# First stage of a four-layer network: five items of the side work move up one step, the sums and taps are dealt out anew

## The reference

```python
u        = layernorm(x_proj)                 # over channels, per token
x_in, z  = split(u @ in_w + in_b)            # 128 and 128 channels
xc       = silu(conv1d_3(x_in))              # three taps along the tokens
dt, B, C = split(xc @ xproj_w)               # 4, 16 and 16 numbers per token
dt       = softplus(dt @ dt_w + dt_b)        # 128 channels
h[n]     = exp(dt * A[n]) * h[n] + (dt * xc) * B[n]     # n = 0..15, a scan over tokens
y        = sum_n C[n] * h[n] + D * xc
out      = (y * silu(z)) @ out_w             # then the 3x3 convolution's half is added, ReLU, residual
```

## Time and profile before

| what | value |
|---|---|
| median of 3 runs | 6879.02 us (6876.97 to 6880.95) |
| span of the profiled execution | 7648.3 us, 89071 instructions |
| own time of the profiled execution | not recorded apart from its span |
| first stage in it, first to last gated product | 141.0 to 2121.3 us |
| busy over the span | TensorE 75%, VectorE 72%, GpSimd 54%, ScalarE 45% |

### The profile page before, as it was taken

The page is one execution under the profiler, slowest core; times in us unless marked ns, Lnnn a source line. Parts: engine busy times, 40 slices in busy tenths (PEclk is TensorE's granted clock), DMA queues, the critical chain, the costliest instruction groups (busy, mean ns, idle before and its releaser), DMA issues. The chain is left out here.

```text
span 7648.3 us, 89071 instructions
## 1 busy us (share of the span) xinstructions
PE 5717.8 (75%) x21147; PEld 3269.1 (43%) x21147; DVE 5490.3 (72%) x12779; ACT 3409.0 (45%) x7221; POOL 4111.0 (54%) x3871
## 2 busy tenths in 40 slices
PE   5999999999989999999865565655656565565442
PEld 2444444444478888888532222322223232232111
DVE  6999999999967777778565666556566665665556
ACT  4888888888855211111233333333333333333333
POOL 4999999999910001000055555655556565565663
PEclk9999999999999999999987676877778777687665
DMA  5445444444420000000156555555555665555567
GB/s 193 170 179 180 167 169 172 170 168 167 168 87 3 3 0 23 0 0 0 42 164 198 164 184 178 168 183 168 180 180 172 193 184 183 178 176 179 178 182 265
DMA packets 306397, 1093.60 MB, mean 143 GB/s; under 512 B 56560, under 2 KB 58639, under 8 KB 264604
## 3 DMA queue, kind: packets, MB, share of 16 engines
q0 software_dynamic: 187440, 625.23, 27.1%
q1 hardware_dynamic: 118516, 464.08, 17.0%
HBM read 997.72 MB, written 91.37 MB: 142 GB/s over the span
## 5 line engine op out<-in xcount | busy, mean ns | idle before, releaser
L1281 POOL DMA_INDIRECT d_ring<-corner_table,d_idx_now x2304 | 2212.2, 960 | 1635.9 <-issue 950.2
L1481 PE MATMUL d_ps_s<-small,d_mix 128*128 128x128 f32 x2304 | 489.6, 350 | 1544.2 <-DVE d_mix L1653 1010.5
L979 POOL TENSOR_TENSOR X<-X 128x512 f32<-128x512 f32 x1024 | 1289.7, 1277 | 168.3 <-DVE X L1017 150.9
L1481 PEld LDWEIGHTS d_ps_s<-small,d_mix 128*128 128x128 f32 x2304 | 327.8, 176 | 2071.0 <-issue 1089.5
L1653 DVE SCALAR_TENSOR_TENSOR d_acc<-d_ring,d_w_now,d_mix 128x128 f32<-128x128 f32 x2304 | 660.9, 354 | 694.3 <-ACT d_mix L1327 321.5
L1017 DVE TENSOR_TENSOR_SCAN X<-X,m_pB 128x512 f32<-128x512 f32 x896 | 1132.4, 1269 | 0.0
L873 PE MATMUL m_pY<-X,small 128*128 128x512 f32 x2048 | 1040.4, 605 | 90.3 <-POOL X L979 90.2
L277 PE MATMUL prop_ps<-prop_parts,prop_w_hi 128*128 128x480 f32 (+4 forms) x4536 | 1099.8, 387 | 4.6 <-DVE prop_parts L286 4.6
L1327 ACT ACTIVATE d_mix<-d_ring,d_w_now 128x128 f32<-128x128 f32 x2304 | 732.3, 390 | 719.1 <-DMA d_ring<-corner_table,d_idx_now 659.1
L277 PEld LDWEIGHTS prop_ps<-prop_parts,prop_w_hi 128*128 128x128 f32 x4536 | 816.0, 188 | 133.4 <-DVE prop_parts L286 5.4
L1411 PE MATMUL d_ps_out<-d_samp,d_dcn_w 128*128 128x512 f32 x1152 | 832.0, 815 | 7.9 <-ACT X L1314 5.8
(11 more groups left out here) (231 smaller groups left out, 7744.8 us busy)
## 6 DMA issues: line engine op xcount, KB each, us to landing
X<-c_scratch SPq DMA_DIRECT2D x256, 1024.0 KB, 4.9
d_ring<-corner_table,d_idx_now POOLq DMA_INDIRECT x2304
corner_table<-d_tT SPq DMA_DIRECT2D x120, 256.0 KB
X<-in_x SPq DMA_DIRECT2D x8, 2048.0 KB, 15.2
m_res<-in_x SPq DMA_DIRECT2D x64, 256.0 KB, 4.6
x_scratch<-m_res SPq DMA_DIRECT2D x64, 256.0 KB, 2.1
x_scratch<-X SPq DMA_DIRECT2D x8, 2048.0 KB
b_x<-x_scratch POOLq DMA_DIRECT2D x16, 1024.0 KB, 11.7
```

Source lines behind the costliest of these rows:

```text
L979: pool.tensor_tensor(hc[:, n % NHC, :], h[:, n, :], Cb[:, n, :], ALU.mult).then_inc(s.HC, 1)
L1281: pool.indirect_dma_start(out=ring[:, m % RING, :], out_offset=None, in_=flat, in_offset=bass.IndirectOffsetOnAxis(ap=idx_now[:, c % 2, m: ...
L1481: turned = pe.transpose(ps_s[k % 3][:, t, :], R[:, k % 3, t, :], G.ident)
```

## The change

Three things are edited, all of them orders; no instruction is added or taken away.

- "log", "softplus", "dt", "dt \* x", and of the layer norm "centre", "variance", "deviation" and "normalise" stand one step earlier on each engine. "pad" stays in step 8 and now comes behind "centre" instead of behind "log".
- The first three taps of the 3x3 convolution move from steps 7, 8, 10 to 6, 7, 9. The others stay at 11, 13 and 15 (the fourth of the six was and is at 11).
- The sums: state 2 from step 6 to 5, state 5 from step 7 to 8, the others as before.

```diff
-        PE_AT = {0: ["tap 0"], 1: ["tap 1"], 2: ["tap 2", "gate input"], 5: ["project B, C", "project dt"], 8: ["centre"],
-                 10: ["variance"]}
-        ACT_AT = {1: ["norm", "halo"], 3: ["silu"], 6: ["dt argument", "round B, C"], 8: ["log", "pad"], 9: ["centre"],
-                  11: ["deviation"]}
-        POOL_AT = {7: ["rest of B, C"], 9: ["softplus"], 10: ["dt"], 11: ["dt * x"], 13: ["normalise"]}
+        PE_AT = {0: ["tap 0"], 1: ["tap 1"], 2: ["tap 2", "gate input"], 5: ["project B, C", "project dt"], 7: ["centre"],
+                 9: ["variance"]}
+        ACT_AT = {1: ["norm", "halo"], 3: ["silu"], 6: ["dt argument", "round B, C"], 7: ["log"], 8: ["centre", "pad"],
+                  10: ["deviation"]}
+        POOL_AT = {7: ["rest of B, C"], 8: ["softplus"], 9: ["dt"], 10: ["dt * x"], 12: ["normalise"]}
         TWO_AHEAD = ("norm", "halo", "centre", "variance", "deviation", "normalise")
-        CONV_AT = {7: 1, 8: 1, 10: 1, 11: 1, 13: 1, 15: 1}
-        SUM_AT = {4: (0, 1), 6: (2, 3), 7: (4, 5), 8: (6,), 9: (7,), 10: (8,), 11: (9,), 12: (10,), 13: (11,), 14: (12,),
+        CONV_AT = {6: 1, 7: 1, 9: 1, 11: 1, 13: 1, 15: 1}
+        SUM_AT = {4: (0, 1), 5: (2,), 6: (3,), 7: (4,), 8: (5, 6), 9: (7,), 10: (8,), 11: (9,), 12: (10,), 13: (11,), 14: (12,),
                   15: (13,)}
         LATE_SUM_AT = {0: 14, 1: 15}
```

## The result

The changed kernel takes 6929.24 us (median of 5 runs, 6921.6 to 6930.49) against 6879.02 us: 50 us more, a ratio of 1.0071 with a 95% interval of 1.0060 to 1.0082. Slower was forecast, with 6929.

A forecast was written before the change was run, and what follows sets the result against it. Bound: a chain closing on itself each chunk over VectorE, GpSimd and TensorE, 31.45 us. Per chunk 0 (softplus side) + 0.80 (normalise) + 0 (ScalarE, taps), times 63 = 50 us; 6879 + 50 = 6929 us, range 6868 to 6962.

The forecast's parts named there:

- The closed loop over w6: One chunk's 31.45 us period: gated product, scan 6, GpSimd's weighing of states 6 to 14, TensorE's last sums, next gated product.
- Faster: Rival, 11%: VectorE's stalls ahead of the gated product are the real limit; 0.64 us a chunk given back, 6839 us.
- Log to dt\*x: Moving log, softplus, dt and dt\*x up one step on ScalarE and GpSimd: gain on the period 0.
- The second product: VectorE's second product of the next chunk: starts 2.25 us after sum 11, now at about 1015.35, its B 1.2 us later.
- VectorE's margin at the gate: VectorE at the gated product by 1020.9, before 1021.97; its delay costs nothing under another 1.0 us.
- Product 15: VectorE's product for state 15: 0.6 us late through the B behind sum 9, held within the 1.2 us of B.
- Normalise, at 0.80 a chunk: On GpSimd, normalise goes before the weighing of state 13, delaying sums 13 to 15 and the gated product: 0.80 us lost.
- The prediction's ends: Bounds of normalise's loss per chunk: 0.83 us, or 0.74 if sum 13, a tap and a B take 1.96 us.
- the second part of the chain: TensorE from sum 14 through tap 0 and one B to sum 15: taken as 2.05 us.
- ScalarE and the taps: Reordered ScalarE items, sum 2 ahead of "project B, C", and taps one step up: delays hidden, cost 0.
- the 769 us between the profile and the median: The profiled execution, 7648.3 us, is 769 us longer than the runs' median; the 50 us were carried over unchanged.
- The clock: Rival, 2%: waits at sums 9, 10, 11 and 13 lower TensorE's clock; 271 us in all, 7150 us and more.

## Why the prediction held

Of the items of side work that moved up, one decides: normalise.

**What sets the period.** The closed loop over w6 held. The gate moved to step 3 shortened it, which an elastic wait would not have shown, and in the changed kernel w6 stayed 7.94 us behind the gate. "Faster" was the rival that took VectorE's stalls for the limit: they went (0.28) or grew (to 1.28), and neither moved the period.

**Log to dt\*x, at 0.** Right: 0.07 a chunk by itself (+3.4 us in all), from the tail behind sum 11. The second product came late by what was said: from sum 11 to it 1033.11 - 1030.86 = 2.25 us. VectorE's margin at the gate was put at 1.0 and was 0.93. Product 15 was put 0.6 late and came 0.64 late (1028.18 - 1007.45 = 20.73 us after the gate against 1009.78 - 989.69 = 20.09), but by another way than described: 0.46 of it had come in at product 13, which waited 0.38 us for its B (1024.46); that B now stands behind "variance".

**Normalise, at 0.80 a chunk.** The mechanism was right and is shown from three sides: the step alone brings the loss, taking it back removes it, a step the other way gains. The size was 0.72 (32.17 - 31.45), and 43.9 us over 63 distances is 0.70, in part because the last distance grew by only 0.17: behind the last chunk neither tap 0 nor a B stands between sums 14 and 15. The prediction's ends were 0.74 and 0.83, so even the lower end was a little high. The term mis-sized is the second part of the chain: I carried over 2.05 us from sum 14 to sum 15, but that held for a sum that starts after a wait (0.96 until the next instruction). Behind a busy queue it is 1.95 (1038.57 - 1036.62), the pipelined 1.96 of the prediction. From sum 13 to sum 14, the part that the prediction's lower end shortened, it stayed 2.05.

**ScalarE and the taps, at 0.** Right for the change as a whole. "Dt argument" waited 0.36 us for its projection (0.5 estimated), and where the side work was for an image's first chunk a scan waited 0.41 for its decay (at 607.27), which did not reach the gate. But the zero for sums and taps holds only beside the rest of the change: dealt out alone they cost 25.8 us, nearly all at the borders. The prediction did not look at the turn of the loop at all.

**The total.** 50 us were forecast and 50.2 measured. The first stage explains 43.9 of them. The last 6 lie within the interval of the ratio and no experiment was made on them. The prediction put all of its 50 us into the first stage, and that grew by 43.9; the other 6 made up for what its 0.80 a chunk was too high, so the exact hit is luck. The sign and the size to within some us are not. That the 769 us between the profile and the median were not in the first stage was an assumption; the traces bear it out.

**The clock.** The granted clock stayed at 1.00 (2.4 GHz) through the stage, with waits of 1.09 us at sum 11; that rival did not occur.

## What to carry to other kernels

When several engines are each busy for 90% of a stage, look for the one chain that closes on itself from period to period, and ask of every moved item only what it is put in front of on that chain. Here an item of 1.23 us that nobody needed early was put in front of w13, on which sum 13, six more queued matmuls and the gate hung; that cost 44 us, and moving it one place the other way was worth 30. A gain in the steady chunk has to be checked at the turn of the outer loop too: five of the orders tried won or kept the period and lost 1.3 to 5.7 us at each turn.

## What the runs showed of the hardware

- A float32 sum that starts after a wait holds up the next matmul for 0.96 us (1034.57 to 1035.53); within a busy queue it is 0.86 (1036.62 to 1037.48).
- Two float32 matmuls of 512 columns on different halves of the 128 rows, one next to the other, take as long as one alone: the low tap with "centre" takes 1.06 us in the changed kernel (1018.57 to 1019.63); split up, the low tap takes 1.05 us by itself, and "centre" again 1.05 (1043.61 to 1044.66).
- At each of the six turns of the loop VectorE stops for 0.7 to 4.3 us and ScalarE for 1 to 4.2 before their first instruction, while the instruction queue moves 6 to 9 blocks; where the loop is entered there is neither. How much of the stop reaches the period depends on the order of work around it: 0.1 us or less at most turns in the kernel before and the changed one, some 4 in that with sums and taps alone. Why the stop's length differs between the orders is open.
- The kernel before took 6879 us where it was measured beside the changed one, and 7615 to 7667 on the three chips of the experiments; whether the chip or the time of the measurement makes the difference is open. The first stage has no part in it: the changed kernel's period is 32.17 us in the trace of 6927 us, and those of its two relatives with normalise at 12 alone and at 11 are the same to 0.01 us in traces of 7675 and 7727. Behind the stage, GpSimd's 2304 indirect DMAs took the same time each (957 and 959 ns), but GpSimd stood idle before them for 879 us in the first of these traces and for 1674 in the last.
